# Four small re-orderings in a two-layer kernel: the routing of tokens to experts, a weight cast on another engine, and a bank rotation

## The chip, the cores and the metric

The kernel runs on one core of a Trainium2 chip. The metric is the device time of one execution, in microseconds (us). Three executions of the kernel before took 1555.25, 1556.9 and 1559.05 us, so the median is 1556.9 us. The engines are named as the profile names them: PE is TensorE (PEld its weight loads), DVE is VectorE, ACT is ScalarE, POOL is GpSimd and SP is SyncE, which here only issues transfers.

## The reference

Two layers with a layer norm after each of four sublayers, on 2048 tokens of width 512. The change touches the third and the fourth sublayer.

```python
def _L1_attn_ref(x, qkv_w, qkv_b, out_w, out_b):        # 2 sequences of 1024, 16 heads of 32
    qkv = x @ qkv_w.T + qkv_b
    ...
    scores = jnp.einsum('bhqd,bhkd->bhqk', q, k) / np.sqrt(D)
    scores = jnp.where(causal, scores, -jnp.inf)
    attn = jax.nn.softmax(scores, axis=-1)
    out = jnp.einsum('bhqk,bhkd->bqhd', attn, v).reshape(b, t, c)
    return out @ out_w.T + out_b

def _L1_ffn_ref(x, router_w, shared_gate, shared_up, shared_down, w_gate, w_up, w_down):
    g = flat @ shared_gate.T                            # inner width 352
    u = flat @ shared_up.T
    shared_out = jax.nn.sigmoid(g) * u @ shared_down.T
    weights = jax.nn.softmax(flat @ router_w.T, axis=-1)     # 8 experts
    top_w, top_idx = jax.lax.top_k(weights, 2)
    ...                                                 # each expert in bf16: sigmoid gate, up, down
    routed = (comb.astype(jnp.bfloat16)[:, :, None] * de).astype(jnp.float32).sum(axis=1)
    return x + shared_out.reshape(Bs, Ss, Hs) + routed.reshape(Bs, Ss, Hs)

x = _layernorm(x + _L1_attn_ref(...), axis=-1)
x = _layernorm(x + _L1_ffn_ref(...), axis=-1)
```

## The kernel before

Every engine has one program, written out in its order by hand; engines meet only at semaphores, and each engine takes its instructions strictly in turn. A product of float32 matrices is done as three matmuls (`product3`, L112 to L117): each operand is split into a high part and a rest, "hi" and "lo", which ACT and DVE (sometimes POOL) make.

**Attention (about 896 to 1253 us).** There are 8 units of four heads. A unit has 12 steps; in each, PE makes four score tiles (L2024, into three banks `st`), ACT takes their exponentials (L1992), POOL clears the part above the diagonal where a step lies on it (L1974, steps 0 to 3 and 8 to 11), and PE adds values and sums two steps later (L2043). Between the scores of unit u, PE also computes the row maxima of later units, 48 "pieces" a unit (`Maxima.piece`, L1357), which DVE reduces (`top`, L1369 and L1372). The pieces go round three banks; bank 0 is also where the finished maxima are transposed (`turn`, step 9), and ACT and DVE read them there (`negate_high` L1387, `negate_low` L1392). Piece 0 of the next unit, in step 10, waits for both. The output projection's weights are split once: the high part by ACT in step 1 of the last unit (`OutWeights.high`, L1705), the rest by DVE (`low`, L1709). At each half of a unit ACT also copies out `den` and `num` (L1983, L1984). POOL casts three pieces of expert weights to bfloat16 in step 4 of each unit (L2160).

**Projection and shared expert (about 1253 to 1396 us).** The tokens go in four blocks i of 512. For each block PE computes gate and up of the shared expert in three column chunks (`shared_gu`, 24 matmuls each); chunk 0 holds the 8 router logits too. The block's input is transposed by PE in four quarters k (`turn`, L2577), two before the third chunk and two inside it, split by ACT (`x_high`) and DVE (`x_low`, L2797). The banks of quarters 0 and 1 are used again for 2 and 3, so `turn(i+1, 2)` waits for DVE's `x_low(i+1)` of quarter 0. ACT's part of a chunk is `shared` (sigmoid, and for chunk 0 the logits); DVE's is `shared` (product and low part). `turn_logits` (L2621) transposes the logits into `dn[1]`, and DVE reads them there.

**Routing, on DVE.** `shift_logits`, then `choose` (softmax, two best experts, marks and running counts `before`), then `place_ranks`, which reads PE's ranks (`rank_tokens`, same bank as the logits) and makes each token's place. After the last block `place_tiles` makes `where` and `sent` [128 x 32 x 39, two of them], `spots` the one-hot tiles, and PE multiplies them (L2702) to get the row numbers with which POOL fetches tokens (L2454). Between these PE does 12 tiles of the shared expert's down product (`early_down`, 9 matmuls each), which DVE adds in (`take_down`). Then 39 expert tiles follow, each beginning with `turn_x` on PE and `take_x` on DVE.

**The start of the fourth sublayer** matters too. POOL's list there is: the last block's layer norm statistics (`root_tiles`, tile by tile), the bfloat16 copy of a block (`x_bf`, L2440) and, behind the second `x_bf`, the low part of the down weights (`sd_lo`, L2448). DVE sets constants (`ones`, `upper`) of which PE makes `iota` (`count_up`, L2672) between the first two chunks. SP sends `x_bf` to memory (`rows`) and loads the next block (`stage`).

## Time and profile before

| what | us |
|---|---|
| median of three executions | 1556.9 |
| lowest, highest | 1555.25, 1559.05 |
| the profiled execution: its time | 1555.22 |
| the profiled execution: its span | 1553.5 |
| PE busy | 1475.8 (95% of the span) |
| DVE busy | 987.2 (64%) |
| ACT busy | 613.9 (40%) |
| POOL busy | 473.9 (31%) |
| mean granted PE clock | 0.986 of full speed |

The span is what the profile's rows cover; 1.7 us of the execution lie around it. PE is the engine with the most work, so the questions are where PE stands idle, on whom it waits there, and where its clock is not the full one.

### The profile page before, as it was taken

How to read it: one execution, taken by the hardware profiler on the slowest of the kernel's cores; microseconds unless marked ns; L12 is line 12 of the kernel's file. 1: busy time of each engine (PE TensorE's matmuls, PEld its weight loads, DVE VectorE, ACT ScalarE, POOL GpSimd, SP SyncE). 2: the span in 40 equal slices, each digit the busy share in tenths (PEclk: the TensorE clock that was granted, in tenths of full speed). 3: DMA queues.
4: the chain of work that ended last, by engine and by line, in shares of the span. 5: the costliest groups of instructions: out<-in, count | busy, mean ns of one | idle time of the engine just before them, and what ended most of it. 6: DMA issues, size and time to landing. Idle time of an engine off the chain costs nothing. (4 is left out here: it accounts for less than half of the span.)

```text
span 1553.5 us, 22540 instructions
## 1 busy us (share of the span) xinstructions
PE 1475.8 (95%) x7696; PEld 1074.8 (69%) x7696; DVE 987.2 (64%) x1905; ACT 613.9 (40%) x1085; POOL 473.9 (31%) x378
## 2 busy tenths in 40 slices
PE   7999889999999999999999999999999898998996
PEld 6788778788888888888887764444444376776554
DVE  6888987845545554553332757777777377567664
ACT  5243355613412431342221135555555635342554
POOL 1233433303421440441342222222222255004760
PEclk9999999999999999999999989999999899999999
DMA  6022347504311430334257683667662655733336
GB/s 216 28 82 79 129 156 247 176 11 144 100 54 41 151 102 4 122 95 164 97 179 227 202 224 105 176 189 196 189 196 101 238 188 187 265 131 129 106 96 230
DMA packets 105228, 223.39 MB, mean 144 GB/s; under 512 B 9328, under 2 KB 35312, under 8 KB 104240
## 3 DMA queue, kind: packets, MB, share of 16 engines
q1 hardware_dynamic: 101392, 211.96, 42.3%
q0 software_dynamic: 3744, 10.23, 2.1%
q8 instruction: 55, 0.90, 0.2%
q14 instruction: 37, 0.30, 0.1%
HBM read 157.54 MB, written 64.36 MB: 143 GB/s over the span
## 5 line engine op out<-in xcount | busy, mean ns | idle before, releaser
L1992 ACT ACTIVATE at_pt<-at_st 128x512 f32<-128x512 f32 (+3 forms) x384 | 164.5, 497 | 147.3 <-PE at_st L2024 146.2
L958 POOL TENSOR_TENSOR ff_w_lo<-ff_raw,ff_w_hi 128x1024 fp32r<-128x1024 f32 x64 | 155.7, 2433 | 206.6 <-ACT ff_w_hi L988 206.6
L115 PE MATMUL op_bank<-ff_x_hi,ff_w_lo 128*128 128x512 f32 x512 | 199.9, 390 | 0.5 <-issue 0.5
L116 PE MATMUL op_bank<-ff_x_lo,ff_w_hi 128*128 128x512 f32 x512 | 199.8, 390 | 0.0
L117 PE MATMUL op_bank<-ff_x_hi,ff_w_hi 128*128 128x512 f32 x512 | 199.7, 390 | 0.0
L1225 DVE TENSOR_TENSOR ff_h_lo<-ff_hf,ff_h_hi 128x512 f32 (+1 forms) x64 | 148.6, 2322 | 53.5 <-ACT ff_h_hi L1113 53.2
L2024 PE MATMUL at_st<-mx_qp,mx_kp 98*128 98x512 f32 (+3 forms) x288 | 104.5, 395 | 13.9 <-ACT at_pt L1992 10.5
L988 ACT ACTIVATE ff_w_hi<-ff_raw 128x1024 fp32r<-128x1024 f32 x64 | 67.8, 1061 | 118.3 <-PE op_bank L117 116.2
L115 PEld LDWEIGHTS op_bank<-ff_x_hi,ff_w_lo 128*128 128x128 f32 x512 | 96.5, 188 | 21.2 <-issue 0.9
L117 PEld LDWEIGHTS op_bank<-ff_x_hi,ff_w_hi 128*128 128x128 f32 x512 | 96.4, 188 | 20.4
L116 PEld LDWEIGHTS op_bank<-ff_x_lo,ff_w_hi 128*128 128x128 f32 x512 | 96.4, 188 | 20.2
L2024 PEld LDWEIGHTS at_st<-mx_qp,mx_kp 98*128 98x128 f32 x288 | 54.7, 198 | 71.4 <-issue 33.7
L115 PE MATMUL mx_mx<-ff_down_hi,ff_h_lo 128*128 128x512 f32 x256 | 100.3, 392 | 0.0
L117 PE MATMUL mx_mx<-ff_down_hi,ff_h_hi 128*128 128x512 f32 x256 | 99.8, 390 | 0.0
L116 PE MATMUL mx_mx<-ff_down_lo,ff_h_hi 128*128 128x512 f32 x256 | 99.6, 389 | 0.0
L1369 DVE CUSTOM_DVE_ANT_0 mx_mx<-mx_mx,mx_mask 128x256 f32<-128x256 f32 (+3 forms) x172 | 82.9, 489 | 22.6 <-PE mx_mx L1357 21.5
L1217 DVE SCALAR_TENSOR_TENSOR ff_hf<-op_bank,ff_sc,ff_hf 128x512 f32<-128x512 f32 x64 | 48.0, 750 | 70.7 <-PE op_bank L117 69.9
L1974 POOL TENSOR_SCALAR_AFFINE_SELECT at_pt<-at_pt 128x512 f32<-128x512 f32 x64 | 41.1, 646 | 156.8 <-ACT at_pt L1992 156.6
L1372 DVE TENSOR_REDUCE mx_tops<-mx_mx 128x1 f32<-128x512 f32 x100 | 68.6, 686 | 23.1 <-PE mx_mx L1357 23.0
L2043 PE MATMUL at_den<-at_pt,at_ones 128*32 128x512 f32 (+3 forms) x768 | 81.6, 497 | 0.0
L1357 PE MATMUL mx_mx<-mx_kp,mx_qp 96*128 96x512 f32 (+1 forms) x208 | 75.4, 370 | 5.9 <-ACT mx_neg_hi L1387 2.4
L1106 ACT ACTIVATE ff_hf<-op_bank,ff_sc 128x512 f32<-128x512 f32 x64 | 44.0, 687 | 84.7 <-PE op_bank L117 84.6
(460 smaller groups left out, 3341.1 us busy)
## 6 DMA issues: line engine op xcount, KB each, us to landing
ff_raw<-in_Wug SPq DMA_DIRECT2D x64, 512.0 KB, 3.6
at_raw<-in_expert_gu SPq DMA_DIRECT2D x16, 704.0 KB, 12.2
mx_qp<-q_hi SPq DMA_DIRECT2D x12, 512.0 KB, 6.4
mx_kp<-k_hi SPq DMA_DIRECT2D x12, 512.0 KB, 11.3
at_raw<-in_expert_d SPq DMA_DIRECT2D x8, 768.0 KB, 13.8
expert_gu_bf<-at_cast SPq DMA_DIRECT2D x16, 352.0 KB, 10.8
ex_e_gu<-expert_gu_bf SPq DMA_DIRECT2D x8, 704.0 KB, 8.4
tm_ln_res<-in_x SPq DMA_DIRECT2D x4, 1024.0 KB, 5.5
```

The costliest lines, as they stand in the source:

```text
L115: pe.matmul(out, cut_l(ll), cut_r(rh), start=first, stop=False, **kw)
L116: pe.matmul(out, cut_l(lh), cut_r(rl), start=False, stop=False, **kw)
L117: return pe.matmul(out, cut_l(lh), cut_r(rh), start=False, stop=last, **kw)
L958: pool.tensor_tensor(w[j][1][:, :, :, :], raw[:, j], f32(w[j][0][:, :, :, :]), ALU.subtract)\
L988: act.activation(w[j][0][:, :, :, :], raw[:, j], ACT.Copy).then_inc(w_hi_ready, 1)
L1225: dve.tensor_tensor(h_lo[:, bass.ds(n + j, 1), :], hf[:, j:j + 1, :], f32(h_hi[:, bass.ds(n + j, 1), :]), ALU.subtract).then_inc(h_lo_read ...
L1357: pe.matmul(bank[:, 0:hi - lo], self.qp[j][0:R_MAX, h, qt * P:(qt + 1) * P], self.kp[j][0:R_MAX, h, lo:hi], start=True, stop=True).then_in ...
L1369: dve.tensor_tensor_reduce(piece, piece, self.mask[:, TB - (hi - lo):], 1.0, -3e38, ALU.add, ALU.max, out)\
L1372: dve.reduce_max(out, piece, AX.X).then_inc(self.piece_read, 1)
L1992: act.activation(pt[:, s % PT, h, off:TB], st[(s * HG + h) % ST][:, off:TB], ACT.Exp, scale=SCALE).then_inc(exp_done, 1)
L2024: pe.matmul(st[(s * HG + h) % ST][:, off:TB], kp[j][0:ROWS, h, kt * P:(kt + 1) * P], qp[j][0:ROWS, h, qc * TB + off:(qc + 1) * TB], start= ...
L2043: mm = pe.matmul(total[rows, off:TB], vv[u % SLOTS][:, kt, rows] if lhs is None else lhs[:, :], pt[:, s % PT, h, off:TB], start=first, sto ...
```

## The change

Seven things, by their place.

1. `OutWeights.high` is done by POOL (`tensor_copy`) in unit 6 behind the three casts, not by ACT in unit 7.
2. A maxima piece n uses bank n+1 of the three (or two, in the opening), so the bank with the transposed maxima is met by piece 2, and the wait for `negate_high` and `negate_low` stands there.
3. At the start of the fourth sublayer POOL does the last layer norm block as tiles 0 to 2 together and then tile 3, both ahead of the first `x_bf`. `sd_lo` is done by DVE, ahead of its constants and behind a wait for the first `x_bf`. SP issues `stage(1)` ahead of `rows(0)`.
4. DVE, blocks 0 to 2: chunk 1's `shared` and the first two quarters of `x_low` come ahead of `choose`, the last two behind it. PE turns quarters 2 and 3 after k = 2 and 3 of the third chunk, not 1 and 2.
5. `place_ranks` is cut in two: `read_ranks`, which frees the bank, comes ahead of the next block's first `shared`. PE's `rank_tokens(i-1)` moves from the end of block i-1 into the first chunk of block i, after k = 1.
6. `sent[:, :, 0]` is done by ACT with a scale per partition (behind the last sigmoid of the shared expert, whose second half waits behind it), `sent[:, :, 1]` by DVE with a `tensor_tensor`; before, DVE did the first with a `tensor_scalar` and POOL the second.
7. PE puts the last `early_down` between `turn_x(0)` and `turn_x(1)`; DVE's `ident_r`, `take_down` and `take_x` follow that order.

```diff
 LayerNorm.scale_act
-        if self.last(i):
-            act.wait_ge(self.shift_ready, (i + t + 1) * 2)
-        elif t == 0:
+        if t == 0:
             act.wait_ge(self.shift_ready, (i + 1) * 2)
+        elif self.last(i) and t == TT - 1:
+            act.wait_ge(self.shift_ready, (i + 2) * 2)
 Maxima.piece (and the same bank in top)
-        bank = self.bank[n % len(self.bank)]
-        if n == 0:
+        bank = self.bank[(n + 1) % len(self.bank)]
+        if n == len(self.bank) - 1:
             at_least(pe, self.neg_hi_ready, u)
             at_least(pe, self.neg_lo_ready, u)
+        if n == 0:
             pe.wait_ge(self.loaded[j], (c + 1) * self.LOADS * DMA)
 OutWeights
-    def high(self, act):
-        act.wait_ge(self.loaded, DMA)
-        act.activation(self.w[0][:, :, :], self.raw[:, :, :], ACT.Copy).then_inc(self.hi_ready, 1)
+    def high(self, pool):
+        pool.wait_ge(self.loaded, DMA)
+        pool.tensor_copy(self.w[0][:, :, :], self.raw[:, :, :]).then_inc(self.hi_ready, 1)
 attend, POOL, in "if s == TT:"
+                        if u == UNITS - 2:
+                            ow.high(pool)
 attend, ACT
-                    if s == OW_STEP:
-                        ow.high(act)
 experts, SP
+        stage(1)
         rows(0)
-        stage(1)
 experts, POOL
-        for t in range(2):
-            out.ln.root_tiles(pool, NB - 1, t, t + 1, NB - 1 + t)
-        pool.wait_ge(sw_lo, 3)
-        pool.wait_ge(out.done, (NB - 1) * TT)
+        out.ln.root_tiles(pool, NB - 1, 0, TT - 1, NB - 1)
+        out.ln.root_tiles(pool, NB - 1, TT - 1, TT, NB)
         for i in range(NB):
             ...
             pool.tensor_copy(x_bf[:, :, :], turned_in[:, :, :]).then_inc(x_bf_ready, 1)
-            if i == 0:
-                for t in range(2, TT):
-                    out.ln.root_tiles(pool, NB - 1, t, t + 1, NB - 1 + t)
-            if i == 1:
-                ...
-                pool.tensor_tensor(sd_lo[:, :, :], raw_d[:, :, :], f32(sd_hi[:, :, :]), ALU.subtract).then_inc(sw_lo, 1)
-                pool.wait_ge(sw_lo, 4)
 ...
-        pool.tensor_tensor(sent[:, :, 1, :], where[:, :, :], ...)
 experts, ACT
+        act.wait_ge(where_ready, 1)
+        act.activation(sent[:, :, 0, :], where[:, :, :], ACT.Copy, scale=place_p[:, 0:1]).then_inc(sent_ready, 1)
+        shared_rest(NB - 1, 2)
 experts, PE
         def after_first(i, k):
             if i == 0 and k == KT - 1:
                 count_up()
+            if i and k == 1:
+                rank_tokens(i - 1)
 
         def after_last(i, k):
-            if i < NB - 1 and k in (1, 2):
-                turn(i + 1, k + 1)
+            if i < NB - 1 and k in (2, 3):
+                turn(i + 1, k)
 ...
-            rank_tokens(i)
 ...
+        rank_tokens(NB - 1)
 ...
-                pe.wait_ge(sd_taken, len(EARLY_DOWN))
+                pe.wait_ge(sd_taken, len(EARLY_DOWN) - 2 + 2 * q)
 ...
         turn_x(0)
+        early_down(len(EARLY_DOWN) - 1)
         turn_x(1)
 experts, DVE
+        dve.wait_ge(sw_hi, 4)
+        dve.wait_ge(sw_lo, 3)
+        dve.wait_ge(x_bf_ready, 1)
+        dve.tensor_tensor(sd_lo[:, :, :], raw_d[:, :, :], f32(sd_hi[:, :, :]), ALU.subtract).then_inc(sw_lo, 1)
         dve.memset(ones[:, :], 1.0).then_inc(consts, 1)
 ...
         for i in range(NB):
+            if i:
+                read_ranks(i - 1)
             shared(i, 0)
             if i:
                 place_ranks(i - 1)
             shift_logits(i)
-            choose(i)
-            shared(i, 1)
             if i < NB - 1:
-                x_low(i + 1)
+                shared(i, 1)
+                x_low(i + 1, (0, 1))
+                choose(i)
+                x_low(i + 1, (2, 3))
                 shared(i, 2)
+            else:
+                choose(i)
+                shared(i, 1)
 ...
-            dve.tensor_scalar(sent[:, :, 0, :], where[:, :, :], place_p[:, 0:1], None, ALU.mult).then_inc(sent_ready, 1)
+            dve.tensor_tensor(sent[:, :, 1, :], where[:, :, :], ..., ALU.mult).then_inc(sent_ready, 1)
```

ACT in steps 0 and 1 of unit 7: `at_pt` are exponentials, the two copies belong to unit 6. Before, and then now:

```order
L1992 ACTIVATE at_pt<-at_st 128x512 x4
L1992 ACTIVATE at_pt<-at_st 128x384 x4
L1983 ACTIVATE at_den_sb<-at_den 128x512
L1984 ACTIVATE at_num_sb<-at_num 128x512
L1705 ACTIVATE ow_w_hi<-ow_raw 128x2048
L1992 ACTIVATE at_pt<-at_st 128x256 x4
```

```order
L1995 ACTIVATE at_pt<-at_st 128x512 x4
L1995 ACTIVATE at_pt<-at_st 128x384 x4
L1986 ACTIVATE at_den_sb<-at_den 128x512
L1987 ACTIVATE at_num_sb<-at_num 128x512
L1995 ACTIVATE at_pt<-at_st 128x256 x4
```

The weight cast of 2048 columns no longer stands between the copies and the next exponentials.

DVE in block 0, from the logits' maximum (`ex_peak`) on; `ex_both` and `ex_before` end `choose`. Before, and then now:

```order
L2812 TENSOR_REDUCE ex_peak<-at_st 128x4
L2814 TENSOR_TENSOR ex_weight<-at_st,ex_peak 128x32
L2831 TENSOR_REDUCE ex_total<-ex_weight 128x4
...
L2855 TENSOR_TENSOR ex_both<-ex_mark 128x32
L2859 TENSOR_TENSOR ex_before<-ex_before,ex_both 128x8 x4
L2804 TENSOR_TENSOR ex_sh_whole<-mx_mx,ex_sh_whole 128x512
L2807 TENSOR_TENSOR ex_sh_lo_7040<-ex_sh_whole,ex_sh_hi_7037 128x512
L2797 TENSOR_TENSOR ex_x_lo<-at_st,ex_x_hi 128x512 x4
```

```order
L2810 TENSOR_REDUCE ex_peak<-at_st 128x4
L2812 TENSOR_TENSOR ex_weight<-at_st,ex_peak 128x32
L2802 TENSOR_TENSOR ex_sh_whole<-mx_mx,ex_sh_whole 128x512
L2805 TENSOR_TENSOR ex_sh_lo_7040<-ex_sh_whole,ex_sh_hi_7037 128x512
L2795 TENSOR_TENSOR ex_x_lo<-at_st,ex_x_hi 128x512 x2
L2829 TENSOR_REDUCE ex_total<-ex_weight 128x4
...
L2853 TENSOR_TENSOR ex_both<-ex_mark 128x32
L2857 TENSOR_TENSOR ex_before<-ex_before,ex_both 128x8 x4
L2795 TENSOR_TENSOR ex_x_lo<-at_st,ex_x_hi 128x512 x2
```

The wide instructions of chunk 1 and of two quarters now stand ahead of the choice, two quarters behind it.

PE at the first expert tile: `ex_x_row` is a fetched tile of tokens, `ex_sd` and `ex_sh` are the operands of `early_down`. Before, and then now:

```order
L117 MATMUL at_num<-ex_sd_hi,ex_sh_hi_7039 128x512
L2719 TENSOR_LOAD ex_owner
L2719 ISA x2
L2714 MATMUL at_st<-ex_ident_b,ex_x_row_7088 128x128 x4
L2714 MATMUL at_st<-ex_ident_b,ex_x_row_7089 128x128 x4
L2729 ISA
L2729 MATMUL mx_mx<-ex_e_gu,ex_x_t_7096 128x352
```

```order
L2716 TENSOR_LOAD ex_owner
L2716 ISA x2
L2711 MATMUL at_st<-ex_ident_b,ex_x_row_7088 128x128 x4
L115 MATMUL at_num<-ex_sd_hi,ex_sh_lo_7042 128x512
L116 MATMUL at_num<-ex_sd_lo,ex_sh_hi_7039 128x512
...
L117 MATMUL at_num<-ex_sd_hi,ex_sh_hi_7039 128x512
L2711 MATMUL at_st<-ex_ident_b,ex_x_row_7089 128x128 x4
```

Nine matmuls of the down product now lie between the two transposes.

## Rows read from the trace of the kernel before

**Rows 1.** Waits of PE, whole span: who waited, total us, times, longest us

```profile
PE at_st L2024 <- ACT at_pt L1992: 12.5, 31, 2.7
PE at_st L2577 <- DVE ex_x_lo L2797: 7.7, 3, 5.5
...
PE mx_mx L1357 <- ACT mx_neg_hi L1387: 3.6, 6, 0.6
...
PE at_st L2702 <- issue: 1.8, 1, 1.8
PE at_st L2621 <- ACT ex_logits_t L2493: 1.5, 1, 1.5
...
PE at_st L2714 <- DVE ex_x_t L3016: 1.3, 1, 1.3
...
PE at_st L2621 <- DVE ex_ranked L2870: 1.2, 3, 0.4
...
PE at_st L2577 <- DMA ex_turned_in<-after_attention: 0.7, 1, 0.7
```

**Rows 2.** Timeline of ACT, start of unit 7: start us, duration us, instruction

```profile
1215.78 1.91 ACT L1705 ACTIVATE ow_w_hi<-ow_raw 128x2048 fp32r<-128x2048 f32 x1
1217.58 1.44 ACT L1992 ACTIVATE at_pt<-at_st 128x256 f32<-128x256 f32 x4
```

**Rows 3.** Windows: engines' busy us, granted PE clock, DMA share, GB/s

```profile
1218.00:1227.20 9.20, 9.18 (x40) 3.31 (x40) 6.01 (x6) 2.00 (x8) 4.64 (x5) 0.50 0.88 331
1299.00:1304.00 5.00, 5.00 (x23) 3.54 (x22) 2.60 (x13) 3.57 (x4) 4.34 (x10) 1.00 0.00 0
1322.30:1326.40 4.10, 4.05 (x15) 3.37 (x15) 0.59 (x1) 0.28 (x1) 0.00 (x0) 0.52 0.98 349
```

**Rows 4.** Timeline of PE in block 0; in brackets idle before and its releaser

```profile
1304.38 0.23 PE L2672 MATMUL at_st<-ex_upper,ex_ones 128*128 128x128 bf16 x1
...
1308.91 0.41 PE L2621 MATMUL at_st<-ex_ident,ex_logits_t 8*128 8x8 f32 x4 [1.46 <-ACT ex_logits_t L2493]
...
1322.35 0.90 PE L2577 MATMUL at_st<-ex_ident,ex_turned_in 128*128 128x128 f32 x3 [5.46 <-DVE ex_x_lo L2797]
```

**Rows 5.** Timeline of DVE, the same two groups in blocks 0 and 1

```profile
1313.08 1.86 DVE L2846 CAST ex_place_f<-ex_place 128x32 f32<-128x32 uint32 x1
...
1315.05 3.56 DVE L2850 TENSOR_TENSOR ex_mark<-ex_iota,ex_place_f 128x32 f32<-128x32 f32 x2
...
1340.73 0.18 DVE L2846 CAST ex_place_f<-ex_place 128x32 f32<-128x32 uint32 x1
...
1341.02 0.29 DVE L2850 TENSOR_TENSOR ex_mark<-ex_iota,ex_place_f 128x32 f32<-128x32 f32 x2
```

**Rows 6.** Timeline of POOL in block 0

```profile
1301.95 1.89 POOL L2440 CAST ex_x_bf<-ex_turned_in 128x2048 bf16<-128x2048 f32 x1
...
1313.02 1.89 POOL L2440 CAST ex_x_bf<-ex_turned_in 128x2048 bf16<-128x2048 f32 x1 [6.10 <-DMA ex_turned_in<-after_attention]
1315.08 3.49 POOL L2448 TENSOR_TENSOR ex_sd_lo<-ex_raw_d,ex_sd_hi 128x1536 fp32r<-128x1536 f32 x1 [0.18 <-POOL ex_x_bf L2440]
```

**Rows 7.** Timeline of DVE, its constants before `count_up`

```profile
1300.76 0.17 DVE L2961 MEMSET ex_ones<- 128x128 bf16 x1
...
1300.88 0.21 DVE L2967 TENSOR_SCALAR ex_upper<-ex_causal 128x128 bf16<-128x128 f32 x1
```

**Rows 8.** Timeline of POOL, unit 6: first mask of its second half

```profile
1200.03 0.63 POOL L1974 TENSOR_SCALAR_AFFINE_SELECT at_pt<-at_pt 128x512 f32<-128x512 f32 x1 [13.23 <-ACT at_pt L1992]
```

**Rows 9.** Tile ex_turned_in: its four loads

```profile
DMA to landing us min/median/max: 5.5/5.6/8.0
```

**Rows 10.** Timeline of DVE behind the last block

```profile
1400.36 1.46 DVE L2917 TENSOR_TENSOR ex_where<-ex_iota,ex_tile_of 128x1248 bf16<-128x1248 f32 x1
1401.86 2.67 DVE L2922 TENSOR_SCALAR ex_sent<-ex_where,ex_place_p 128x1248 bf16<-128x1248 bf16 x1
```

**Rows 11.** Instructions of L2454, the fetches of tokens: durations ns, first and last start

```profile
L2454 POOL DMA_INDIRECT ex_x_row<-expert_rows,ex_row_from x39: 942/970/1243, 1409.9 to 1506.1; - x39
```

More of the change, by code:

```diff
@@ L1366, in top @@
         out = self.tops[:, h, qt:qt + 1] if lo == 0 else self.tops2[:, h, qt - TT:qt - TT + 1]
-        piece = self.bank[n % len(self.bank)][:, 0:hi - lo]
+        piece = self.bank[(n + 1) % len(self.bank)][:, 0:hi - lo]
         if hi == (qt + 1) * P:
@@ L2440, in on_gpsimd @@
             pool.tensor_copy(x_bf[:, :, :], turned_in[:, :, :]).then_inc(x_bf_ready, 1)
-            if i == 0:
-                for t in range(2, TT):
-                    out.ln.root_tiles(pool, NB - 1, t, t + 1, NB - 1 + t)
-            if i == 1:
-                pool.wait_ge(sw_hi, 4)
-                pool.wait_ge(sw_lo, 3)
-                pool.wait_ge(x_bf_ready, 2)
-                pool.tensor_tensor(sd_lo[:, :, :], raw_d[:, :, :], f32(sd_hi[:, :, :]), ALU.subtract).then_inc(sw_lo, 1)
-                pool.wait_ge(sw_lo, 4)
         def fetch(q):
@@ L2461, in send @@
                                     y_row[q % YRING][:, :], None).then_inc(y_out[q % YRING], DMA)
-        pool.wait_ge(where_ready, 1)
-        pool.tensor_tensor(sent[:, :, 1, :], where[:, :, :],
-                           entry[:, :].rearrange("p (n o) -> p n o", o=1).to_broadcast([P, ENTRIES, TILES]),
-                           ALU.mult).then_inc(sent_ready, 1)
         pool.wait_ge(rows_stored, NB * TOPK * DMA)
@@ L2490, in shared, with shared_rest @@
             act.activation(sh[0:rows, s, :], gate[s][0:rows, :], ACT.Sigmoid).then_inc(sig_ready, 1)
+            if c < NB * NM - 1:
+                shared_rest(i, pos)
+        def shared_rest(i, pos):
+            c, m = i * NM + pos, ORDER[pos]
+            rows, s = MC[m], c % 2
             if pos == 0:
@@ L2704, in on_tensor @@
         mm.then_inc(sent_done, 1)
-        for n in range(8, len(EARLY_DOWN)):
+        for n in range(8, len(EARLY_DOWN) - 1):
             early_down(n)
@@ L2860, in choose, with read_ranks @@
                     .then_inc(before_ready, 1)
-        def place_ranks(i):
+        def read_ranks(i):
             tiles = slice(i * TT, (i + 1) * TT)
@@ L2870, in place_ranks @@
             dve.tensor_tensor(ranked2[:, :, :], ranks_in, mark[:, 0, tiles, :], ALU.add).then_inc(ranks_read, 1)
+        def place_ranks(i):
+            tiles = slice(i * TT, (i + 1) * TT)
             settle()
@@ L2921, in place_tiles @@
             dve.wait_ge(where_ready, 1)
-            dve.tensor_scalar(sent[:, :, 0, :], where[:, :, :], place_p[:, 0:1], None, ALU.mult).then_inc(sent_ready, 1)
+            dve.tensor_tensor(sent[:, :, 1, :], where[:, :, :],
+                              entry[:, :].rearrange("p (n o) -> p n o", o=1).to_broadcast([P, ENTRIES, TILES]),
+                              ALU.mult).then_inc(sent_ready, 1)
         def place_owners():
@@ L3000, in on_vector @@
                 spots(i - 1)
+        read_ranks(NB - 1)
         place_ranks(NB - 1)
@@ L3006, in on_vector @@
         place_owners()
-        for n in range(4, len(EARLY_DOWN)):
+        for n in range(4, 10):
             take_down(n)
@@ L3011, in on_vector @@
         dve.wait_ge(he_clear, 2)
+        dve.tensor_copy(ident_r[:, :], ident[:, :]).then_inc(ident_r_ready, 1)
         def take_x(q):
@@ L3029, in res_low @@
                 dve.tensor_tensor(low, whole, f32(res_hi[t][:, :]), ALU.subtract).then_inc(res_lo_ready, 1)
-        dve.tensor_copy(ident_r[:, :], ident[:, :]).then_inc(ident_r_ready, 1)
+        take_down(10)
         take_x(0)
+        take_down(11)
         take_x(1)
```

## The prediction

> **What bounds the kernel now.** I read the page's first part, then the waits of PE over the whole span, then the timelines of PE, DVE, ACT and POOL at each place that the diff touches, then windows for the clock. PE is busy for 95% of the span, so only two things can give time back: moments in which PE waits, and stretches in which it works at the half clock. The waits [rows 1] put a number on what the change aims at: 7.7 us on `x_low`, 2.7 us of one wait on the exponentials, 3.6 us in six waits for the negated maxima, 1.8 us ahead of the `sent` product, 1.5 us for the logits, 1.3 us for `take_x`, 1.2 us in three waits for the ranks to be read, 0.7 us for a block's load.
>
> The clock is the second thing. Behind the 2.7 us wait of unit 7 PE is granted 0.50 for 9.2 us, in which it is busy 9.18 us; that is the level of 1.2 GHz, half of 2.4. Behind the longest wait on `x_low` it is granted 0.52 over 4.1 us, with 4.05 us busy [rows 3]. At the full clock that work takes about half: 4.6 us and 2.0 us are lost there beside the idle time.
>
> **Part 1, the weight cast.** ACT's cast stands at 1215.78 us for 1.91 us, and the exponentials that PE waits for start only at 1217.58 [rows 2]. Without it they start at 1215.78: 1.8 us less. PE's wait shrinks from 2.7 to 0.9 us. Does the clock then hold? Waits of 1.5 us and 1.8 us [rows 1] are followed by no stretch below the full clock, so I take yes: another 4.6 us. Bounds: 1.8 us if the clock falls all the same, 6.4 us if not. The cast on POOL should take what the equally wide `x_bf` cast takes, 1.89 us [rows 6]; POOL is idle for 13.23 us between its casts of unit 6 and the next mask [rows 8], and would hold PE up only if the cast took more than that. Its cost is 0. DVE's `low` then runs in its idle time ahead of unit 7. I take 6.4.
>
> **Part 2, the banks.** Six waits of 0.6 us [rows 1]. Pieces 0 and 1 and one score tile now go ahead of piece 2, which still waits for `negate_low`. That is about 0.3 us of PE work (half of a wait); DVE gets its first piece earlier by the same. Bounds: 0 (the time comes back as a wait for DVE, which reads six pieces in a row there) and 3.6. I take 6 x 0.3 = 1.8.
>
> **Parts 3 and 4, blocks 0 to 2.** In block 0 two things meet. DVE's cast and marks take 1.86 and 3.56 us there, against 0.18 and 0.29 in block 1 [rows 5]. They lie exactly under POOL's `x_bf` cast (1313.02 to 1314.91) and `sd_lo` (1315.08 to 1318.57) [rows 6]: DVE stands still until POOL is done. That is 1.68 + 3.27 = 4.95 us, and most of the 5.46 us which PE waits for `x_low` [rows 4]. The Trainium skill (SBUF — State Buffer, "Who interferes with whom") says that a DVE instruction with two SBUF inputs, or in a two-port mode, and a GpSimd instruction exclude each other for the whole instruction; the trace agrees to 0.1 us. By this rule the new order is not free either: a cast on POOL can still meet a two-input instruction on DVE.
>
> With `sd_lo` gone from POOL and two quarters of `x_low` ahead of `choose`, the quarter that PE wants is there early. My chain for block 0: chunk 1 ends on PE about 1312.5, ACT's sigmoid behind its table loads about 1313.3, product, high and low part until 1315.4, two quarters until 1316.7; PE, now turning one k later, wants the first (done at 1316.1) at 1317.5. The margin is 1.4 us. POOL's second `x_bf`, 1.89 us [rows 6], may fall on DVE's low part of chunk 1 in this stretch and use that up; in the chain above it ends before, because the load lands earlier. So the waits of 5.5 us (block 0) and 2 x 1.1 (blocks 1 and 2, together 7.7) go, and the 2.0 us at the half clock with them: 9.7.
>
> The logits' wait of 1.5 us goes: ACT's last layer norm tiles are no longer behind the first `x_bf`. The load's 0.7 us goes: issued ahead of `rows(0)` it should land in 5.6 us rather than 8.0 [rows 9], some 2 us before PE wants it. The three rank waits, 1.2 us, go with `read_ranks`. Sum 3.4.
>
> What is added: `sd_lo` on DVE waits for the first `x_bf`. That ended at 1303.84 [rows 6] and now comes 0.4 us later, since all four tiles' statistics go first: 1304.25. The instruction itself: `where`, two inputs, 1248 columns, 1.46 us [rows 10], so for 1536 columns 1.8 us; POOL's own 3.49 us is the upper bound, nothing is below 1.46. It ends at 1306.05. Behind it are queued the constants, which took 0.33 us from `ones` to the end of `upper` [rows 7]; `count_up` on PE needs them and stood at 1304.38 [rows 4]. Now it starts at about 1306.4: a new wait of 2.0 us (bounds 1.7 and 3.7), with chunk 1 of PE queued behind it. I subtract 2.0.
>
> Does that new wait drop the clock? The nearest rows stand on both sides: 1.8 us without a drop, 2.7 us with one [rows 1, 3]. The Trainium skill (TensorE: Matmul & The Clock Gate, "What's actually happening") tells it as a gate that halves the clock behind an idle stretch and lifts it after sustained work, independent of where the kernel is; by that rule 2.0 us may be enough in some executions and not in others. From the rows a drop costs between 2.0 and 4.6 us; I take no drop and keep that cost for a rival.
>
> Net of parts 3 and 4 with the ranks: 9.7 + 3.4 - 2.0 = 11.1.
>
> **Part 5, where the waits for the ranks could come back.** `rank_tokens(i-1)` now stands 12 matmuls into block i. 23 matmuls fall in 5.0 us [rows 3], so that is 2.7 us behind the block's start, and `choose` by my chain (3.4 us behind 1316.7, the length that it has in block 1) ends at about 1320.2, when PE starts block 1. It has 2.7 us to spare. Cost 0.
>
> **Part 6, `sent`.** DVE's `tensor_scalar` took 2.67 us beside POOL's second half; the same shape as `where` with two inputs and nothing on POOL is 1.46 us [rows 10]. ACT's half, 1248 columns, by its cast of 2048 in 1.91 us [rows 2] is about 1.2 us, and is done sooner than DVE's. `spots`, and PE's product behind it, come 1.2 us sooner; PE's wait of 1.8 us becomes 0.6. Bounds 0 and 1.8; I take 1.2.
>
> **Part 7, the first expert tiles.** The wait of 1.3 us for `take_x` lies under nine matmuls now. The first fetch is issued at 1409.9 [rows 11] and starts with the row numbers, so it moves with the 1.2 us; PE wants it 2.1 us earlier relative to them than before. If it is late PE stalls with nothing else to do: bounds -2.1 and +1.3. I take 1.3.
>
> **Sum.** 6.4 + 1.8 + 11.1 + 1.2 + 1.3 = 21.8. The profiled execution took 1555.2 (span 1553.5 and 1.7 around it), so it becomes 1533.4; the median of the runs is 1.7 higher, 1556.9 - 21.8 = 1535.1. A wait's row counts only the idle time; restarting behind each of a dozen stalls costs a little more, so I name 1534.5.
>
> **The rivals.**
> First, the clock. Either it falls in unit 7 in spite of the shorter wait, or the new wait at `count_up` drops it. For it: 2.0 us lies between the cases seen. Against: everything near is shorter than what dropped it. Time: 1534.5 + 4.6 = 1539, with both 1543. Chance 0.2.
>
> Second, the cover in blocks 0 to 2 fails: `shared(i, 1)` on DVE now waits for ACT's sigmoid, which stands behind two table loads, and `x_low` behind that. For it: in blocks 1 and 2 `place_ranks` still comes ahead of the logits' shift and so of the exponential. Against: the margin above. The 2.2 us of blocks 1 and 2 stay, and about 4 us more comes back: 1541. Chance 0.1.
>
> Third, more than forecast: all 3.6 us of part 2, all of the `sent` wait, `count_up` shorter than I think: 1534.5 - 1.8 - 0.6 - 1 = 1531. Chance 0.1. That parts 2 and 7 do nothing at all is in my own range (3 us).
>
> Fourth, slower. One mechanism: `choose` behind the wide work is late for `rank_tokens` in the middle of a block. It decides from a delay of more than the 2.7 us to spare, which takes a `choose` of 8 us as in block 0 before (5.0 us longer, rows 5), in each of blocks 0 to 2, through POOL's casts. Then PE stalls 2.4 us in each block, and each stall drops the clock at 4.6 us: 3 x 7.0 = 21; with `count_up` dropping it too, 1534.5 + 21 + 4.6 = 1560. Against: only the cast of 1.89 us is left on POOL in each block. Chance 0.02.
>
> **How the numbers follow.** Forecast 0.58, with its own range 1531 to 1538. The range for 8 in 10 takes in the third case and most of the first and second: 1530 to 1541. About 0.2% (3 us) is what a measurement of this kernel can tell from no change. Only the fourth case and remnants of the others reach that far: faster 0.96, same 0.02, slower 0.02.
>
> **What would show it.** The weights' cast on POOL in unit 6 at about 1.9 us, and no stretch at 0.50 in unit 7. DVE's cast and marks in block 0 at 0.2 and 0.3 us. No wait of `turn` on `x_low`; one wait of `count_up` (L2667) on DVE of about 2 us, and a granted clock of 1.00 behind it. A wait of about 0.6 us ahead of the `sent` product. The waits for `mx_neg_hi` at 0.3 us or replaced by ones on `mx_tops`. Wrong it would be made by a half clock in the blocks, by `rank_tokens` waiting for `ex_before`, or by `turn_x(0)` waiting for its fetch.

## The result, and the profile after

The change makes the kernel faster: 1539.4 us (median of 4 executions, 1538.0 to 1542.4) against 1557.3 us (4 executions), 17.9 us less. The ratio, estimated over all executions and not from the two medians (whose ratio is 0.9885), is 0.9893, 95% interval 0.9876 to 0.9909, which is 14 to 19 us. The forecast was 21.8 us by its sum; the time lies inside the range and 5 us above the number named, 1534.5. The profiled execution has a span of 1537.9 us, 15.6 less than before, and a mean granted clock of 0.988.

The waits of PE over the whole span, as in [rows 1]: who waited for whom, us in total, times, longest.

```profile
PE at_st L2025 <- ACT at_pt L1995: 11.1, 33, 1.0
PE mx_mx L1358 <- DVE mx_tops L1370: 4.4, 12, 0.5
PE at_st L2667 <- DVE ex_upper L2975: 2.0, 1, 2.0
PE mx_mx L1358 <- DVE mx_tops L1373: 1.9, 6, 0.3
PE mx_mx L1358 <- issue: 1.5, 6, 0.2
PE at_st L2699 <- issue: 0.6, 1, 0.6
```

The 7.7 us on `x_low`, the 1.5 on the logits, the 1.2 on the ranks, the 0.7 on a load and the 1.3 on `take_x` are gone. The `sent` wait is 0.6 and the new wait of `count_up` 2.0, both as forecast. The six waits on `mx_neg_hi` (3.6 us) are gone too, but a row "issue" of 1.5 us is new and that on `mx_tops` (L1370) is 4.4 us where it was 2.3: 3.6 us again.

Where the time went, by landmarks in the two timelines (start of each `mx_neg_hi` on ACT, then of PE's first product of the projection, first `ex_sg_lo`, `count_up`, `sent`, the second `turn_x`, and PE's first product with `ex_y_in` behind the expert tiles). Stage lengths in us; the last four columns are experiments told below. "First unit" is the stretch between the first two `mx_neg_hi`, and "unit 7" the one behind the eighth.

| stage | before | after | e3 | e7 | e9 | e10 |
|---|---|---|---|---|---|---|
| start to the first maxima in attention | 902.3 | 900.8 | 902.1 | 904.9 | 902.4 | 904.0 |
| first unit | 48.4 | 48.5 | 48.7 | 47.5 | 48.9 | 47.4 |
| the next six units, each | 42.3 | 42.3, two 43.9 | 41.5, one 41.8 | 42.3, one 43.9 | 42.3, two 43.9 | 41.5, one 41.8 |
| unit 7, up to the projection | 48.0 | 44.0 | 42.4 | 42.4 | 42.4 | 42.4 |
| projection | 46.1 | 46.1 | 46.1 | 46.1 | 46.1 | 46.1 |
| first `ex_sg_lo` to `count_up` | 5.6 | 7.7 | 7.7 | 5.6 | 7.7 | 5.6 |
| `count_up` to `sent` | 101.8 | 88.2 | 86.6 | 86.8 | 86.6 | 86.8 |
| `sent` to the second `turn_x` | 11.3 | 9.9 | 9.9 | 9.9 | 9.9 | 9.9 |
| expert loop | 112.8 | 112.9 | 138.0 | 136.2 | 136.1 | 135.8 |

Before to after: -1.5 ahead of attention, which no edit touches except for the rotation; +3.1 in the units, -4.0 in unit 7, -11.5 from `ex_sg_lo` to `sent`, -1.4 from there to the second `turn_x`. Together -15.3; the rest of the 15.6 lies behind the expert loop.

Three readings. First, clock. Windows of the kernel after, columns as in [rows 3]: the stretch that was at 0.50 in unit 7, then two that are below the full clock now.

```profile
1217.90:1227.10 9.20, 8.43 (x73) 3.63 (x77) 3.71 (x5) 5.09 (x14) 3.94 (x4) 1.00 1.03 419
1229.30:1233.10 3.80, 3.80 (x17) 0.87 (x17) 1.29 (x2) 2.45 (x5) 0.00 (x0) 0.56 1.06 404
1304.10:1307.90 3.80, 3.77 (x10) 2.96 (x11) 2.83 (x12) 1.21 (x2) 0.00 (x0) 0.55 0.92 314
```

A window in one of the two units of 43.9 us:

```profile
1076.90:1083.00 6.10, 5.49 (x24) 1.91 (x25) 4.92 (x14) 0.99 (x3) 2.08 (x4) 0.72 0.07 23
```

The 9.2 us are at the full clock now. But there is a short stretch near the half clock behind a wait of 0.96 us in the same unit, and one behind `count_up`; two more lie in the units of 43.9 us. Each costs 1.5 to 1.6 us, by the same stage in profiles without it (43.9 against 42.3, 44.0 against 42.4, 88.2 against 86.6). The cast on POOL, and PE's two waits in unit 7 (the first was 2.7 us before):

```profile
1188.37 1.90 POOL L1706 CAST ow_w_hi<-ow_raw 128x2048 fp32r<-128x2048 f32 x1
```

```profile
1217.83 0.38 PE L2025 MATMUL at_st<-mx_qp,mx_kp 98*128 98x256 f32 x1 [0.93 <-ACT at_pt L1995]
1229.29 0.79 PE L2025 MATMUL at_st<-mx_qp,mx_kp 98*128 98x512 f32 x1 [0.96 <-ACT at_pt L1995]
```

Second, the banks. PE and then DVE at the turn of the maxima, one unit (start us, duration us; in brackets the idle time and who ended it):

```profile
1034.61 0.42 PE L1358 MATMUL mx_mx<-mx_kp,mx_qp 96*128 96x384 f32 x1 [0.24 <-issue]
1035.67 0.50 PE L1358 MATMUL mx_mx<-mx_kp,mx_qp 96*128 96x512 f32 x1 [0.53 <-DVE mx_tops L1370]
```

```profile
1034.23 0.28 DVE L1393 SCALAR_TENSOR_TENSOR mx_neg_lo<-mx_mx,mx_neg_hi 32x128 fp32r<-32x128 f32 x1 [3.51 <-ACT mx_neg_hi L1388]
1034.44 0.93 DVE L2070 RECIPROCAL at_den_sb<-at_den_sb 128x128 f32<-128x128 f32 x1
1035.30 0.26 DVE L1370 CUSTOM_DVE_ANT_0 mx_mx<-mx_mx,mx_mask 128x128 f32<-128x128 f32 x1
```

PE starts its second piece at 1034.09, but DVE reads the first at 1035.30, because a reciprocal of 0.93 us stands behind `negate_low`. The fourth piece, which takes that bank again, waits for it. Ahead of `negate_low` DVE had been idle for 3.51 us.

Third, block 0. DVE's cast and marks, which took 1.86 and 3.56 us [rows 5]:

```profile
1318.88 0.18 DVE L2844 CAST ex_place_f<-ex_place 128x32 f32<-128x32 uint32 x1
1319.17 0.29 DVE L2848 TENSOR_TENSOR ex_mark<-ex_iota,ex_place_f 128x32 f32<-128x32 f32 x2
```

And PE at `count_up`, which was at 1304.38 with no wait [rows 4]:

```profile
1304.13 0.23 PE L2667 MATMUL at_st<-ex_upper,ex_ones 128*128 128x128 bf16 x1 [2.00 <-DVE ex_upper L2975]
1304.17 0.64 PE L115 MATMUL mx_mx<-ex_x_hi,ex_sg_lo 128*128 128x512 f32 x1
```

The 0.64 us of the matmul behind it, instead of about 0.40, is the half clock.

### The profile page after: what moved, and what is told of

Same layout as the page of the kernel before. It is cut to its first block and busy times, and to the rows that moved or that the text cites. A ratio compares the mean times of both kernels' runs of the same rounds, so it can differ in the third digit from the quotient of the medians.

```text
span 1537.9 us, 22528 instructions
## 1 busy us (share of the span) xinstructions
PE 1472.8 (96%) x7696; PEld 1073.0 (70%) x7696; DVE 982.8 (64%) x1906; ACT 613.5 (40%) x1085; POOL 469.8 (31%) x369
## 5 line engine op out<-in xcount | busy, mean ns | idle before, releaser
L1370 DVE CUSTOM_DVE_ANT_0 mx_mx<-mx_mx,mx_mask 128x128 f32<-128x128 f32 (+2 forms) x200 | 101.7, 518 | 21.5 <-PE mx_mx L1358 20.7
L1551 POOL TENSOR_TENSOR qkv_part_lo<-qkv_whole,qkv_part_hi 128x512 fp32r<-128x512 f32 x32 | 42.7, 1334 | 89.7 <-ACT qkv_part_hi L1566 81.0
## 6 DMA issues: line engine op xcount, KB each, us to landing
mx_kp<-k_hi SPq DMA_DIRECT2D x12, 512.0 KB, 11.3
expert_gu_bf<-at_cast SPq DMA_DIRECT2D x16, 352.0 KB, 10.9
```

Source lines behind the costliest of these rows:

```text
L1370: dve.tensor_tensor_reduce(piece, piece, self.mask[:, TB - (hi - lo):], 1.0, -3e38, ALU.add, ALU.max, out)\
```

## The experiments

Each is compared with the kernel before in the same session. In these sessions the expert loop took 134 to 138 us in every kernel, also in those that leave it as it was, where the first comparison had 113: the kernel before took 1577 to 1578 us. PE waits there 14 to 19 us for `ex_he_t` (0.7 in the first comparison). Its cause was not followed. The three sessions ran on three chips. So a ratio and the stage lengths are read, not a time across sessions. A ratio given here is estimated from all executions; that of the medians can differ by about 0.001 (e1: 0.9904 and 0.9916).

**e1, the rotation undone** (in `piece`, and for the same bank in `top`).

```diff
-        bank = self.bank[(n + 1) % len(self.bank)]
-        if n == len(self.bank) - 1:
+        bank = self.bank[n % len(self.bank)]
+        if n == 0:
             at_least(pe, self.neg_hi_ready, u)
```

> The changed kernel with the maxima pieces back on their old banks (part 2 undone, all else kept). The changed kernel's ratio to the kernel before is 0.9893 (1539.4 against 1557.3). Theory A: the rotation gained nothing, because DVE starts to read pieces only behind its reciprocal of 0.93 us, and PE's six waits of 0.6 us for mx_neg_hi only became six of 0.24 and six of 0.53 behind it; the unit's cadence was 42.33 us before and is 42.33 after. Then undoing it changes nothing beyond chance: ratio 0.988 to 0.991, the waits for mx_neg_hi back at 6 x 0.6 and those for mx_tops (TENSOR_TENSOR line) down by about 2 us. Rival B: the rotation's two waits per unit are what lets the clock fall (two stretches of 3.4 us at half clock in the attention units, 1.5 us each, which the kernel before does not have); then undoing it is 3 us faster, ratio 0.987, and no such stretch between 940 and 1200 us. Rival C: the rotation does gain 0.3 us a unit: 2 us slower, 0.991.

Measured: ratio 0.9904, interval 0.9888 to 0.9921; whole units 42.3 us, and again two of 43.9. The waits:

```profile
PE mx_mx L1357 <- ACT mx_neg_hi L1387: 3.6, 6, 0.6
PE mx_mx L1357 <- DVE mx_tops L1369: 2.3, 12, 0.2
```

Theory A: alone, the rotation only renames 3.6 us of waiting. B falls: the long units are there without it. C falls by the units and not by the ratio, whose interval holds 0.991 as well. One thing more: the first unit takes 44.7 us here and not 48.4, because the stretch of 10.2 to 13.7 us at half clock, which all twelve other profiles have there, is absent behind the same wait of 3.10 us.

**e2, the constants ahead of `sd_lo`.**

```diff
-        dve.wait_ge(sw_hi, 4)
-        ...
-        dve.tensor_tensor(sd_lo[:, :, :], raw_d[:, :, :], f32(sd_hi[:, :, :]), ALU.subtract).then_inc(sw_lo, 1)
         dve.memset(ones[:, :], 1.0).then_inc(consts, 1)
         ...
         dve.tensor_scalar(upper[:, :], causal[:, :], -1.0, None, ALU.is_lt).then_inc(consts, 1)
+        dve.wait_ge(sw_hi, 4)
+        ...
+        dve.tensor_tensor(sd_lo[:, :, :], raw_d[:, :, :], f32(sd_hi[:, :, :]), ALU.subtract).then_inc(sw_lo, 1)
```

> The changed kernel with DVE's constants (ones to upper) ahead of sd_lo. They then run in DVE's idle time before 1302 us, and count_up on PE need not wait. Theory A: the 2.0 us wait for ex_upper goes, and with it the stretch of 3.4 us at half clock right behind it (1.5 us): 3.3 to 3.5 us faster than the changed kernel, 1536 us, ratio 0.987; no PE wait between 1298 and 1330 us, no half clock there. Rival B: the clock falls there whatever the wait (a stretch of half clock remains in block 0): only 2.0 us, ratio 0.988. Rival C: sd_lo under it makes iota, the entries and the first product late, and the time comes back as a wait of PE in chunk 1 or on x_low: no gain, 0.989.

Measured: 0.9883, interval 0.9865 to 0.9901; too wide to tell from the change alone, so the trace decides. `ex_sg_lo` to `sent` took 94.0 us against 95.9 in the kernel after, and 94.3 in e3, which has the 2.0 us wait and full clock behind it. So the 2.0 us wait is gone and only 0.3 us are won: two waits came up in its place. DVE, POOL and PE in block 0:

```profile
1311.09 1.56 DVE L2805 TENSOR_TENSOR ex_sh_lo<-ex_sh_whole,ex_sh_hi 128x512 fp32r<-128x512 f32 x1 [0.77 <-ACT ex_sh_hi L2495]
```

```profile
1310.21 1.89 POOL L2439 CAST ex_x_bf<-ex_turned_in 128x2048 bf16<-128x2048 f32 x1 [9.20 <-DMA expert_rows<-ex_x_bf]
```

```profile
1313.31 0.66 PE L2572 MATMUL at_st<-ex_ident,ex_turned_in 128*128 128x128 f32 x4 [0.65 <-DVE ex_x_lo L2795]
```

The low part of chunk 1 takes 1.56 us instead of 0.69, since it begins under POOL's cast; `x_low` behind it is late for PE by 0.65 us. The other, 0.62 us, is for the load of block 2. This is what the forecast had named as the danger of a margin of 1.4 us; in the change itself the 2.0 us wait hides it. So rival C, in its x_low form, with a load besides. The stretch at half clock is absent too, but so it is in e3 and e9, which have the 2.0 us wait; that it went because of the edit is not shown.

**e3, the reciprocal ahead of `negate_low` in step 9.**

```diff
+                if s == TURN_STEP:
+                    invert(u, 0, s - DIVIDE_FIRST)
                 if s == TURN_STEP and u + 1 < UNITS:
                     mx.negate_low(dve, u + 1)
 ...
-                if 0 <= s - DIVIDE_FIRST < DIVIDE_CHUNKS:
+                if s != TURN_STEP and 0 <= s - DIVIDE_FIRST < DIVIDE_CHUNKS:
```

> The changed kernel with one edit on DVE: in step 9 the reciprocal of 128 columns (0.93 us) stands ahead of negate_low, where DVE idles 3.5 us, and not behind it. Theory A: the reciprocal is what delays DVE's first reads of the next pieces, so PE's wait for piece 0 to be read (0.53 us in each of 6 units) goes and a unit takes 41.8 us instead of 42.33: 3 us faster, and if the clock no longer falls in the attention units another 3 us: ratio 0.9855 to 0.9875 against 0.9893. Rival B: DVE reads pieces in a row there and is the bound of the step, the wait for the tops moves to a later piece or to the exponentials: unit at 42.3 us, ratio 0.989 to 0.990.

Measured: 0.9863, interval 0.9843 to 0.9882, units of 41.5 us, none longer than 41.8. ACT's `mx_neg_hi` in two successive units, the kernel after and then e3:

```profile
991.60 0.27 ACT L1388 ACTIVATE mx_neg_hi<-mx_mx 32x128 fp32r<-32x128 f32 x1 [1.45 <-PE mx_mx L1383]
1033.93 0.27 ACT L1388 ACTIVATE mx_neg_hi<-mx_mx 32x128 fp32r<-32x128 f32 x1 [1.45 <-PE mx_mx L1383]
```

```profile
992.31 0.27 ACT L1388 ACTIVATE mx_neg_hi<-mx_mx 32x128 fp32r<-32x128 f32 x1 [1.45 <-PE mx_mx L1383]
1033.80 0.27 ACT L1388 ACTIVATE mx_neg_hi<-mx_mx 32x128 fp32r<-32x128 f32 x1 [1.45 <-PE mx_mx L1383]
```

42.33 and 41.49 us, so 0.8 us in each of six units. Theory A. Behind its wait of 2.01 us at `count_up` the clock stays full, which is also worth the 1.5 us by which its `count_up` to `sent` is shorter.

```profile
1296.30:1300.10 3.80, 3.76 (x19) 2.90 (x20) 2.83 (x12) 1.20 (x2) 0.00 (x0) 1.00 0.95 313
```

**e4, part 1 alone on the kernel before** (the cast on POOL, nothing else).

> The kernel before with part 1 alone: the weights' cast on POOL in unit 6, not on ACT in unit 7. The recorded forecast gave this part 6.4 us (1.8 idle, 4.6 half clock): 1550.9, ratio 0.9959. Theory A, from the trace of the changed kernel: PE's wait at the start of unit 7 shrinks to 0.9 us and the clock holds there, but some 11 us on, behind the wait of 0.96 us that ACT's copies of den and num cause, comes a shorter stretch of 3.4 us at half clock: 4.0 us gained, ratio 0.9974. Rival B: the late stretch is chance and does not come: 6.4 us or a little less, 0.996. Rival C: POOL's cast disturbs DVE or the next mask in unit 6: under 2 us, 0.999 or more.

Measured: 0.9977, interval 0.9967 to 0.9987, which is 3.6 us (2.1 to 5.2). In its profile unit 7 takes 42.4 us, 5.6 less than before, with the full clock throughout; an earlier unit is a long one (43.9 us). So part 1 is worth 5.6 us in unit 7 when the clock holds and 4.0 when, as in the kernel after, a short stretch below it follows. The forecast's 6.4 lies outside the interval. That interval holds the chance stretches of all stages; it is the 42.4 us of unit 7, the same in all eight profiles with this part and no such stretch in that unit, that sizes the part.

**e5, part 4 alone on the kernel before** (the order of `choose` and `x_low`, and PE's quarters one k later; `sd_lo` still on POOL, the ranks still at the block's end).

> The kernel before with part 4 alone: chunk 1 and two quarters of x_low ahead of choose in blocks 0 to 2, and PE's quarters 2 and 3 one k later. sd_lo stays on POOL. Theory A (DVE and POOL exclude each other): the low part of chunk 1 (two SBUF inputs) now falls under POOL's x_bf or sd_lo (until about 1318.6 us) and is stretched as the marks were; PE's wait for x_low in block 0 shrinks from 5.5 to about 2 us, the 2 x 1.1 us of blocks 1 and 2 go: 5.5 to 8 us faster, ratio 0.995 to 0.9965. Rival B (no exclusion, only the order mattered): all of 7.7 and 2.0 us go, ratio 0.9938. Rival C (the order is worth nothing without the cast's move): under 3 us, 0.998 or more.

Measured: 0.9974, interval 0.9964 to 0.9984, which is 4.1 us (2.5 to 5.7), less than theory A's 5.5 at least. The stage did what A said: `count_up` to `sent` falls from 101.8 to 94.5 us, 7.3 less. What lies between the two was not settled; this profile has a longer opening (905.6 us) and one long unit. No wait on `x_low` is left. POOL, then DVE:

```profile
1316.16 3.75 POOL L2448 TENSOR_TENSOR ex_sd_lo<-ex_raw_d,ex_sd_hi 128x1536 fp32r<-128x1536 f32 x1 [0.18 <-POOL ex_x_bf L2440]
```

```profile
1317.30 0.69 DVE L2797 TENSOR_TENSOR ex_x_lo<-at_st,ex_x_hi 128x512 fp32r<-128x512 f32 x1 [0.77 <-ACT ex_x_hi L2482]
1318.69 0.69 DVE L2797 TENSOR_TENSOR ex_x_lo<-at_st,ex_x_hi 128x512 fp32r<-128x512 f32 x1 [0.70 <-ACT ex_x_hi L2482]
```

`x_low`, one of whose two inputs is in PSUM (`at_st`), runs its usual 0.69 us in the midst of POOL's `sd_lo`. Only instructions with nothing in PSUM were held: the cast, the marks, the low part in e2. One input is enough for that: in e4 the comparison that makes `upper` took 1.89 us under the first `x_bf`, where it takes 0.21 [rows 7]. POOL, then DVE:

```profile
1297.31 1.89 POOL L2440 CAST ex_x_bf<-ex_turned_in 128x2048 bf16<-128x2048 f32 x1
```

```profile
1297.39 1.89 DVE L2967 TENSOR_SCALAR ex_upper<-ex_causal 128x128 bf16<-128x128 f32 x1
```

But not every one with nothing in PSUM: in the kernel before, the layer norm's statistics (`BATCH_NORM_STATS2`, 512 columns, L202 at 1296.13) took 0.70 us under a POOL subtraction of 3.25 us. The Trainium skill (SBUF — State Buffer, "Who interferes with whom") says that a DVE instruction with at most one SBUF input, outside the two-port modes, does not contend with GpSimd; the trace agrees, for `x_low` and for the statistics. In return PE waits for the ranks, which part 5 moves away:

```profile
1322.65 0.18 PE L2629 MATMUL at_st<-ex_both,ex_upper 128*128 128x32 bf16 x1 [1.04 <-DVE ex_both L2855]
```

The same in blocks 1 and 2 at 1.26 and 1.00 us. The low part of chunk 1 fell between POOL's two instructions (0.82 us), so theory A's 2 us wait did not come; the three rank waits (3.3 us, where they were 1.2) take most of the 2.4 us by which B's 9.7 is more than the stage gave.

**e6, `sd_lo` on DVE alone**, behind the constants, on the kernel before.

> The kernel before with one edit: sd_lo is done by DVE (1536 columns, 1.8 us, behind its constants and the first x_bf) and not by POOL. Theory A (exclusion): DVE's marks in block 0 take 0.3 us and not 3.56; the cast in front of them still lies under x_bf (1.9 us). PE's wait for x_low in block 0 falls from 5.5 to about 2.2 us, and the stretch at half clock behind it may go: 3.3 to 5.3 us faster, ratio 0.9966 to 0.9979; the waits of 1.1 us in blocks 1 and 2 stay. Rival B: the marks were slow for another reason: under 1 us, 0.9995.

Measured: 0.9996, interval 0.9983 to 1.0009: no gain. The marks do take 0.29 us now and the wait on `x_low` in block 0 falls from 5.5 to 3.1 us, with the clock still at 0.50 for 6.8 us behind it. What POOL's cast holds in block 0 is now a product of `choose`, `ex_weight`, 1.82 us instead of 0.19. And the wait for the logits grows to 2.8 us; it was 1.5 in the kernel before, but 0.4 and 0.3 in e4 and e5, which leave that stretch as it was. DVE, then POOL:

```profile
1305.67 1.76 DVE L2965 TENSOR_TENSOR ex_sd_lo<-ex_raw_d,ex_sd_hi 128x1536 fp32r<-128x1536 f32 x1 [2.78 <-POOL ex_x_bf L2440]
```

```profile
1305.92 1.95 POOL L228 TENSOR_TENSOR at_ln_rstd_all<-at_ln_rstd_all,at_ln_half 128x1 f32<-128x1 f32 x1
1308.85 0.57 POOL L228 TENSOR_TENSOR at_ln_rstd_all<-at_ln_rstd_all,at_ln_half 128x1 f32<-128x1 f32 x1
```

The lock works the other way too: POOL's layer norm step takes 1.95 us under DVE's `sd_lo`, 0.57 free of it, and ACT's scaling and then the logits wait for it. A's mechanism is right, its sum wrong. B gave the right number for the wrong reason. By these rows, moving `sd_lo` pays only if the layer norm tiles go ahead of `x_bf`, as in the change; no run has those two edits alone.

**e7, e2 with two more edits**: in blocks 0 to 2 chunk 1's low part goes behind two quarters of `x_low`, and the load of `res[0]` behind `stage(2)`.

```diff
             if i < NB - 1:
                 shared(i, 1)              # without its low part
                 x_low(i + 1, (0, 1))
+                shared_low(i, 1)
                 choose(i)
 experts, SP
-        sp.dma_start(res[0][:, :, :], src_t[:, 0:TT, :]).then_inc(res_loaded[0], DMA)
         for i in range(1, NB):
             rows(i)
             if i < NB - 1:
                 stage(i + 1)
+            if i == 1:
+                sp.dma_start(res[0][:, :, :], src_t[:, 0:TT, :]).then_inc(res_loaded[0], DMA)
```

> The changed kernel with the constants ahead of sd_lo as in e2, where two waits of PE came up behind the one removed: 0.65 us on x_low (the low part of chunk 1 took 1.56 us, not 0.69, under POOL's second x_bf) and 0.62 us on the load of block 2. So two more edits: in blocks 0 to 2 the low part of chunk 1 goes behind the two quarters of x_low, and SP issues the load of res[0] behind stage(2). Theory A: both waits go, x_low (one input in PSUM) is not held by POOL: 1.3 us faster than e2, ratio 0.987 to 0.9875 against 0.9883, stretch from the first projection chunk (ex_sg_lo) to the sent product 92.5 us against 94.0 in e2 and 95.9 in the changed kernel. Rival B: x_low is held by POOL's cast as the low part was: the wait of about 0.6 us on x_low stays: 0.9878.

Measured: `ex_sg_lo` to `sent` 92.4 us, as A said (e2 94.0), and PE has no wait from there up to the 0.76 us ahead of `sent` itself. The ratio is 0.9894, interval 0.9878 to 0.9911, so the executions do not show that gain over the change or e2: it is 1.6 us against intervals of 2.5 us on either side, and its profile has a long unit and a longer opening (904.9 us). Shown in the stage, not in the time.

**e8, e7 with the reciprocal of e3.**

> e7 with the reciprocal ahead of negate_low as in e3. Theory A: the gains add up. e3 saved 0.8 us in each of 7 units and the chance stretches at half clock there; with the 3.3 us of e7 the stage times add to about 8 us less than the changed kernel: ratio 0.984. Rival B: they don't add, because the clock falls elsewhere when PE runs closer to its others: 0.986 as e3 alone.

Measured: 0.9846, interval 0.9833 to 0.9859; units of 41.5 us, 92.4 us to `sent`, no long unit.

**e9, the change again; e10, e8 again; e11, e8 with the old banks.** One session, so that they stand side by side.

> The changed kernel itself, once more, on the chip on which the next two run, as their base. Theory A: the gain on the kernel before is that of the stage times, 16 to 18 us, and the short stretches at half clock fall on other places than in its first profile, because they are chance: 0 to 2 in the seven attention units, perhaps none behind the 2.0 us wait of count_up; ratio 0.988 to 0.991. Rival B: the stretches are fixed by the program: again one in each of the fifth and sixth whole unit, one in unit 7 and one behind count_up.

Measured: 0.9898, interval 0.9881 to 0.9914 (1562.0 us). Two units of 43.9 us, but the third and fourth of the seven (the first unit counted) and not the fifth and sixth; none of the short stretches in unit 7, and none behind the 2.02 us wait of `count_up`. A: they move from execution to execution.

> e8 once more, beside the changed kernel. Theory A: its stage times in the traces are shorter than those of the changed kernel by 5.5 to 6 us in the attention units and by 2 to 3.5 us between the first projection chunk and the sent product: 7.5 to 10 us faster than the changed kernel on the same chip, ratio to the kernel before 0.983 to 0.985. Rival B: the kernels meet again behind the expert loop, whose time rises by what was saved in front of it: less than 4 us faster.

Measured: 0.9828, interval 0.9809 to 0.9847 (1551.1 us): 10.9 us less than e9 in the same session, and its interval lies wholly below. This is the fastest version tried; it beats both kernels. Not all of the 10.9 us is the edits' own: in the two profiles the six units give 4.7 us and the stretch to `sent` 1.9; that e10 has no long unit (3.1 us) and a shorter stretch at half clock in the first unit (1.4 us) may be chance in part, and its opening was 1.6 us longer.

> e8 with the maxima pieces back on their old banks: the reciprocal stays ahead of negate_low. Theory A: with DVE's reads no longer late, PE's wait for the negated maxima is what is left in that step, so the rotation is worth about 0.3 us a unit now, as the recorded forecast had it: the unit takes about 41.8 to 41.9 us, not 41.5; 2 to 2.5 us slower than e10. Rival B: the reciprocal alone makes the gain, and the rotation is worth nothing here either: unit 41.5 us, same time as e10.

Measured: 0.9851, interval 0.9831 to 0.9871 (1554.3 us), units of 42.1 us:

```profile
994.70 0.27 ACT L1387 ACTIVATE mx_neg_hi<-mx_mx 32x128 fp32r<-32x128 f32 x1 [1.45 <-PE mx_mx L1382]
1036.75 0.27 ACT L1387 ACTIVATE mx_neg_hi<-mx_mx 32x128 fp32r<-32x128 f32 x1 [1.46 <-PE mx_mx L1382]
```

By the means over the six whole units, with the reciprocal out of the way the rotation is worth 0.5 us a unit (42.07 against 41.56), and without the rotation the reciprocal is worth 0.27 (42.34 against 42.07). The rotation is worth nothing without the other edit; together they give 0.8. The medians differ by 3.2 us, which the overlapping intervals alone would not prove; the units do.

## Why the prediction was mostly right, and where 6 us went

Forecast 21.8 us, found 15.6 in the profiled execution, part by part:

- **Part 1** was forecast at 6.4 us and gave 4.0. The mechanism was right: the wait fell from 2.7 to 0.93 us and the 9.2 us behind it ran at the full clock. Two sizes were off. At the full clock PE catches up with ACT and meets three small waits there again (0.20, 0.28 and 0.28 us), so 6.4 was 5.6 (unit 7 at 42.4 us in e2 to e4 and e7 to e11). And in this execution a short stretch below the full clock took 1.6 back.
- **Part 2** was forecast at 1.8 and gave 0. The failed step is "DVE gets its first piece earlier by the same". I counted only the reads in a row, and named their coming back as the lower bound; the row of DVE that mattered, the reciprocal between `negate_low` and the first read, I had not looked at. The engine that is waited for has a queue of its own. With the reciprocal moved the rotation gives 0.5 us a unit (e11 against e10), more than the 0.3 that I took and less than the upper bound of 0.6.
- **Parts 3 to 5** were forecast at 11.1. The stretch to `sent` is 11.5 shorter, 1.2 of it part 6, so 10.3; without the stretch at half clock behind `count_up` it would be 11.8. All the waits named went, and the new one was 2.00 us where 2.0 was worked out. The cast on POOL that might use up the margin did so only once the 2.0 us were gone (e2). One term rests on a single profile: the wait of 1.5 us for the logits was 0.4 us in e4. Its stretch to `sent` was 107.1 us all the same, against 107.4, because more of PE's work fell under the half clock behind `x_low`.
- **Part 6** was forecast at 1.2, and the wait is 0.6 as worked out. **Part 7**: 1.3 forecast, 1.4 found, with no wait for a fetch. Parts 5, 6 and 7, and of part 3 the layer norm tiles and the order of the loads, have no run of their own; their worth is read from the waits in the traces.
- **The clock.** Rival one priced a fall at 4.6 us and tied it to long waits. It did come, but in other pieces: stretches of 1.5 to 1.6 us, four of them in this execution, 6.2 us together. One of the kernel before in the opening (1.7 us) was absent after, so the net is about 4.5. That, the 1.8 of part 2 and the 0.8 of part 1, less 0.8 by which the other parts gave more, is what was missing. The measured 1539.4 is also the first rival's 1539, but that is luck: it had one fall of 4.6 us in mind. Of the signs that the forecast named, the waits came as said; the full clock behind `count_up` did not (0.55), and a half clock in the blocks was one of the signs of being wrong.

What the clock depends on stays partly open. The same waits recur in the profiles, and how often a stretch near the half clock begins during them or within 2.1 us of their end can be counted:

| wait of PE | profiles that have it | with such a stretch |
|---|---|---|
| 5.5 or 3.1 us, block 0 (before, e4, e6) | 3 | 3 |
| 3.1 us, first unit (on `ones`) | 13 | 12 |
| 2.7 us, unit 7 (before, e5, e6) | 3 | 3 |
| 2.0 us, `count_up` (after, e1, e3, e9) | 4 | 2 |
| 0.96 us, unit 7 where the clock held behind the 0.93 us | 10 | 2 |

So the forecast's two nearest rows, 1.8 us without a drop and 2.7 us with one, left out that one wait can do either. The Trainium skill (TensorE: Matmul & The Clock Gate, "What's actually happening") tells of a gate set by how busy PE has been recently; that one and the same place falls in some executions and holds in others agrees with it. It puts the fall behind idle stretches, and does not say that waits as short as these are enough: the forecast's "by that rule 2.0 us may be enough" is not in it, and rests on these executions alone.

In attention, with units of 42.3 us, 12 of 54 whole units in nine profiles had such a stretch, though no single wait there is over 0.6 us. All twelve began 2.8 to 3.4 us behind the start of the unit's `mx_neg_hi`, which is where the waits of the turn lie: which unit has one is chance, where in the unit is not. With units of 41.5 us (e3, e8, e10) it was 0 of 18, and in e11, which keeps the wait of 0.6 us but has 2.1 us of idle time in a unit and not 2.3, 0 of 6. So less idle time in the step seems to end them. That is a count over profiles; no experiment varied the idle time by itself, and the length of the unit changed with it.

## What to carry to other kernels

When a wait is to be taken away, read the queue of the engine that ends it, between its last instruction and the one that PE will need next: a 0.9 us reciprocal there made a bank rotation worth nothing, and moving it into an idle gap made the two together worth 0.8 us a unit. Price what a new wait hides as well: removing it (e2) brought up two others. Where GpSimd works beside DVE, put the DVE instructions with an input in PSUM into its shadow, and those with both inputs in SBUF, casts and comparisons with a constant outside it. And read a wait that a forecast leans on from more than one profile: the logits' wait was 1.5 us in one and 0.3 to 0.4 us in two others.
